# A five-stage transformer kernel: experts with four chunks in flight, and attention's constants and first loads made in earlier stages

## The reference, cut to what matters

```python
mod = (silu(L0_c) @ L0_wmod)            # six rows of 256 per sequence: shift, scale, gate, twice
x = x + ga * attention(layernorm(x) * (1 + ca) + sa)   # 16 heads of 16, ALiBi bias, causal
x = x + gb * fp4_swiglu(layernorm(x) * (1 + cb) + sb)
mod = (silu(L1_c) @ L1_wmod)
x = x + ga * state_space(layernorm(x) * (1 + ca) + sa)
h = layernorm(x) * (1 + cb) + sb
# experts: six of rank 16, the two with the largest softmax weight are used
base_out, shared_out = h @ base_W.T + base_b, (h @ shared_A.T) @ shared_B.T
gate = softmax(h @ router_W.T + router_b)            # [.., 6]
sparse_w = top2(gate) / (sum(top2(gate)) + 1e-6)
routed = sum_e sparse_w[e] * (h @ routed_A[e].T) @ routed_B[e].T
x = x + gb * (base_out + shared_out + routed)
```

## Time and profile before

| what | value |
|---|---|
| median of three runs | 4541.62 us (4540.84 to 4541.89) |
| the profiled execution | 4536.81 us, its span 4535.0 us |
| setup | 0 to 37.6 us |
| projection | 37.6 to 249.1 us |
| attention | 249.1 to 1416.9 us |
| experts | 4219.6 to 4535.0 us |
| TensorE busy over the span | 78% |
| VectorE busy | 79% |
| GpSimd busy | 53% |
| ScalarE busy | 50% |

### The profile page before, as it was taken

How to read it: one execution, slowest core, us unless ns; L and a number is a source line. 1 busy time by engine, 2 the same in 40 slices (tenths; PEclk the granted TensorE clock), 3 DMA queues, 4 the chain that set the end, 5 groups by cost and what they waited for, 6 DMA issues and landing times. The chain is left out here.

```text
span 4535.0 us, 73462 instructions
## 1 busy us (share of the span) xinstructions
PE 3538.0 (78%) x23500; PEld 1707.1 (38%) x23500; DVE 3567.3 (79%) x5194; ACT 2248.1 (50%) x3972; POOL 2406.5 (53%) x1812
## 2 busy tenths in 40 slices
PE   6949999999995899999567777777777777775566
PEld 3614444444442555555222222222222222221455
DVE  4767777777773899999289999989998999999344
ACT  3606666666664333333365665556565666564111
POOL 1120000000000788887278888888888888888121
PEclk8969999999997899999778888888887888885777
DMA  4864545545532111110112222222222122222111
GB/s 155 279 111 61 79 63 74 79 63 75 78 44 56 52 47 42 46 43 26 47 38 58 64 63 57 61 65 56 56 63 64 54 53 52 55 52 56 50 59 53
DMA packets 274028, 300.57 MB, mean 66 GB/s; under 512 B 34559, under 2 KB 204662, under 8 KB 273622
## 3 DMA queue, kind: packets, MB, share of 16 engines
q1 hardware_dynamic: 273630, 295.68, 29.7%
HBM read 210.22 MB, written 84.51 MB: 65 GB/s over the span
## 5 line engine op out<-in xcount | busy, mean ns | idle before, releaser
L1648 POOL TENSOR_TENSOR d_dBu<-d_dtu,d_Bn 128x1024 f32<-128x1024 f32 x512 | 1202.5, 2374 | 185.7 <-DVE d_h L1715 185.5
L749 DVE TENSOR_REDUCE b_Gc<-b_pS 128x1 f32<-128x512 f32 (+4 forms) x1248 | 748.8, 645 | 297.1 <-PE b_pS L630 189.2
L1496 ACT ACTIVATE d_dA<-d_dt,d_decay 128x512 f32<-128x512 f32 x1024 | 690.3, 687 | 448.7 <-DVE d_h L1715 431.9
L712 ACT ACTIVATE b_P<-b_pT 128x512 f32<-128x512 f32 (+1 forms) x1120 | 583.3, 575 | 397.5 <-PE b_pT L618 233.7
L1715 DVE TENSOR_TENSOR_SCAN d_h<-d_dA,d_dBu 128x512 f32<-128x512 f32 x512 | 586.2, 1204 | 96.9 <-ACT d_dA L1496 85.2
L1715 DVE TENSOR_TENSOR_SCAN d_h<-d_dA,d_last_h,d_dBu 128x512 f32<-128x512 f32 x512 | 616.5, 1264 | 54.7 <-ACT d_dA L1496 50.2
L584 POOL CAST b_gp<-b_gT 32x128 bf16<-32x128 f32 x32 | 9.0, 280 | 1032.3 <-ACT b_gT L696 1032.3
L628 PE MATMUL b_pS<-b_KS,b_QS 99*128 99x512 bf16 (+3 forms) x1536 | 473.4, 338 | 89.6 <-DMA b_V<-scratch_v 64.3
L616 PE MATMUL b_pT<-b_QS,b_KS 102*128 102x512 bf16 (+3 forms) x1536 | 470.7, 330 | 37.3 <-issue 20.9
L1722 DVE TENSOR_TENSOR d_h<-d_h,d_C 128x2048 f32<-128x2048 f32 x192 | 434.3, 2262 | 0.5 <-PE d_C L1379 0.5
L1451 PE MATMUL d_f<-d_xnT,w_inT 128*128 128x512 f32 x512 | 327.1, 773 | 128.0 <-DVE d_h1e L1782 59.8
(11 more groups left out here) (294 smaller groups left out, 6253.5 us busy)
## 6 DMA issues: line engine op xcount, KB each, us to landing
d_Bn<-scratch_bs SPq DMA_DIRECT2D x64, 1024.0 KB, 8.2
scratch_parts<-a_part SPq DMA_DIRECT2D x48, 512.0 KB, 4.0
b_QS<-scratch_parts SPq DMA_DIRECT2D x192, 128.0 KB, 7.0
b_KS<-scratch_parts SPq DMA_DIRECT2D x192, 128.0 KB, 7.3
scratch_v<-a_v SPq DMA_DIRECT2D x16, 1024.0 KB, 7.4
b_V<-scratch_v SPq DMA_DIRECT2D x32, 512.0 KB, 11.1
a_x<-in_L_attn_x_dram SPq DMA_DIRECT2D x16, 512.0 KB, 7.5
scratch_o<-b_O SPq DMA_DIRECT2D x16, 512.0 KB, 10.8
```

Of the source, the lines that this page charges most:

```text
L712: act.activation(t[:, heads[0]:heads[-1] + 1, c * CH:c * CH + w], pT[:, place % RING, 0:len(heads) * w].rearrange("p (h w) -> p h w", w=w) ...
L749: dve.tensor_reduce(Gc[:, m.k % 2, c, :].rearrange("p (h t) -> p h t", t=QT)[:, heads[0]:heads[-1] + 1, qt], pS[:, j % RING, 0:len(heads) ...
L1496: act.activation(dA[:, m % 2, :], dt[:, c.k % 2, m, :], ACT.Exp, scale=decay[:, m, n:n + 1]).then_inc(dA_d, 1)
L1648: pool.tensor_tensor(dBu[:, n % 2, 2 * j:2 * j + 2, :], dtu[:, c.k % 2, 2 * j:2 * j + 2, :], Bn[:, n // BG % 2, n % BG, :].unsqueeze(1).to ...
```

## The change

It has two parts, in stages that are far apart.

**Attention's constants and first loads.** `QS`, `KS`, `V` and `alp` are allocated ahead of `setup`. In `setup` SyncE loads the table between the loads of `c` and `wmod`, VectorE splits it, and ScalarE writes the ones (two copies of 6 partitions by 16384 elements). In `project_qkv`'s second step, behind the load of chunk 2, SyncE issues the 12 transfers from `alp` to `KS`. In its last step, ahead of the last chunk's stores, SyncE issues the 13 transfers of unit 0. `attend` starts with the load of unit 1.

```diff
--- setup
+            sp.dma_start(al[:, :], A["alibi"]).then_inc(al_in, 16)
+            act.wait_ge(one_set, 1)
+            for rows in (K["QS"], K["KS"]):
+                rows = rows[NROW:KROWS, :, :, :].rearrange("p g h t -> p (g h t)")
+                act.activation(rows, one[NROW:KROWS, :].to_broadcast(rows.shape), ACT.Copy).then_inc(ones, 1)
--- project_qkv, SyncE's step
                 if f is not None and (not isinstance(f.base, int) or f.base * U + f.k + 1 < total):
                     load(At(f.base, U, f.k + 1))
+                if f is not None and isinstance(f.base, int) and f.base == 0 and f.k == 1:
+                    for g_ in range(NG):
+                        for p in range(NPART):
+                            sp.dma_start(K["KS"][NROW + p:NROW + p + 1, g_, :, :], K["alp"][g_ * HG * QT:(g_ + 1) * HG * QT, p, :]).then_inc(S["alp_put"], 16)
+                if f is None and g is None:
+                    for sl in range(2):
+                        sp.wait_ge(stored[sl], 64)
+                    load_unit(sp, S, K, 0, 0)
--- attend
-            sp.wait_ge(ones, 2)
-            sp.wait_ge(al_step, 5)
-            for g in range(NG):
-                for p in range(NPART):
-                    sp.dma_start(KS[R0 + p:R0 + p + 1, g, :, :], alp[g * NQ:(g + 1) * NQ, p, :]).then_inc(alp_put, 16)
-                if u is None and m.k == 0:
-                    load(m)
-            pool.memset(QS[R0:KROWS, :, :, :].rearrange("p g h t -> p (g h t)"), 1.0).then_inc(ones, 1)
-            pool.memset(KS[R0:KROWS, :, :, :].rearrange("p g h t -> p (g h t)"), 1.0).then_inc(ones, 1)
```

```diff
+        LAG_G, LAG_D, LAG_C = 1, 2, 3
+        def chunks(step):
+            for s in range(total + LAG_C):
+                step(*(s - lag if 0 <= s - lag < total else None for lag in (0, LAG_G, LAG_D, LAG_C)))
--- TensorE: transposes of hw(c), transposes of xn(g), output products of c, hidden products of g
+                if c is not None:
+                    wait(pe, hw_d, 2 * c + 2)
+                    wait(pe, hwT_d, c)
...
+                    last.then_inc(hw_tr, 1)
+                if g_ is not None:
+                    wait(pe, xn_d, g_ + 1)
+                    wait(pe, hT_d, g_)
...
+                    last.then_inc(tr_d, 1)
+                if c is not None:
+                    wait(pe, hwT_d, c + 1)
+                    wait(pe, og_d, c)
...
+                    last.then_inc(o_mm, 1)
+                if g_ is not None:
+                    wait(pe, hT_d, g_ + 1)
+                    wait(pe, hw_d, 2 * g_ - 2)
...
+                    last.then_inc(a_mm, 1)
--- ScalarE: Exp of d, hwT of c, xn of f
+                if d is not None:
+                    wait(act, soft, NSOFT * (d + 1))
+                    act.activation(ex[:, d % 2, :, :], lg[:, :, :], ACT.Exp).then_inc(ex_d, 1)
+                if c is not None:
+                    wait(act, hw_tr, c + 1)
+                    wait(act, o_mm, c - 1)
+                    act.activation(hwT[:, c % 2, :], p_hw[0:NHW, :], ACT.Copy).then_inc(hwT_d, 1)
```

More of the change, by code:

```diff
@@ L1858, in _ @@
-            chunks(sp, step)
-            for i in range(4):
-                sp.wait_ge(stored[i], 16 * total // 4)
+                wait(sp, stored[n % XS], n // XS * 16)
+                sp.dma_start(x[:, n % XS, :, :], S["x3"][n * CH:(n + 1) * CH, :].rearrange("(t p) d -> p t d", p=P)).then_inc(x_in[n % XS], 16)
+                if n % 2 == 0:
+                    wait(sp, og_d, n - 2 * (GS - 1))
+                    sp.dma_start(gate[:, n // 2 % GS, :], S["mod"][n // 2:n // 2 + 1, 1, GB, :].to_broadcast([P, D])).then_inc(g_in[n // 2 % GS], 16)
@@ new lines, in step @@
+            def step(f, g_, d, c):
+                if f == 0:
+                    load(0)
+                    load(1)
+                if f is not None and f + 2 < total:
+                    load(f + 2)
+                if c is not None:
+                    wait(sp, out_d, c + 1)
+                    sp.dma_start(out[c * CH:(c + 1) * CH, :].rearrange("(t p) d -> p t d", p=P), x[:, c % XS, :, :]).then_inc(stored[c % XS], 16)
+            chunks(step)
+            for i in range(XS):
+                sp.wait_ge(stored[i], 16 * total // XS)
@@ L1862, in _, with step @@
         @block.tensor
         def _(pe):
-            def step(a, c):
-                if a is not None:
-                    wait(pe, xn_d, a.times(1, 1))
-                    wait(pe, hT_d, a.times(1, 0))
+            def step(f, g_, d, c):
+                if c is not None:
+                    wait(pe, hw_d, 2 * c + 2)
+                    wait(pe, hwT_d, c)
+                    for t in range(CT):
+                        last = pe.transpose(p_hw[0:NHW, t * P:(t + 1) * P], hw[:, c % 2, t, :], K["ident"][:, :])
+                    last.then_inc(hw_tr, 1)
+                if g_ is not None:
+                    wait(pe, xn_d, g_ + 1)
+                    wait(pe, hT_d, g_)
@@ L1912, in _, with step @@
-            chunks(act, step)
+            chunks(step)
         @block.gpsimd
         def _(pool):
-            pool.wait_ge(const, 9)
-            def step(a, c):
-                if a is not None:
-                    sl = a.k % 2
-                    wait(pool, stat, a.times(2, 2))
-                    wait(pool, xn_d, a.times(1, -1))
+            pool.wait_ge(const, 8)
+            def step(f, g_, d, c):
+                if f is not None:
+                    sl = f % 2
+                    wait(pool, stat, 2 * f + 2)
+                    wait(pool, xn_d, f - 1)
@@ L2010, in _ @@
-            chunks(dve, step)
+                if d is not None:
+                    wait(dve, ex_d, d + 1)
+                    picked(dve.tensor_reduce(sm[:, :], ex[:, d % 2, :, :], AX.X, ALU.add))
+                    pick_wait()
+                    picked(dve.reciprocal(sm[:, :], sm[:, :]))
+                    pick_wait()
+                    picked(dve.tensor_tensor(g[:, :, 0:NE], ex[:, d % 2, :, :], tiles(sm[:, :], NE), ALU.mult))
+                if g_ is not None:
+                    b = g_ // 2
+                    wait(dve, tr_d, g_ + 1)
+                    wait(dve, o_mm, g_ - HS_ + 1)
+                    dve.tensor_scalar(hT[:, g_ % HS_, 0, :], p_tr[:, 0, :], K["cb1"][:, 0, b:b + 1], K["sb1"][:, 0, b:b + 1], ALU.mult, ALU.add)
```

268 lines of the change are left out of this document (124 added, 144 removed).

## The result

The changed kernel takes 4375.98 us (median of 4 runs, 4365.23 to 4378.46), the kernel before 4541.23 (4 runs, 4534.00 to 4541.89). The ratio is 0.9635, with a 95% interval of 0.9616 to 0.9654: 165 us less, where 163 were predicted, and inside the range.

What follows compares the result with a forecast made beforehand. No engine bounds the two places: attention's start is a serial chain, an experts step a chain of dependencies. Experts -122.2, attention's start -41.4, setup +0.5 make -163.1 us; from 4541.6 that gives 4378.5, rounded to 4379, range 4359 to 4413.

Steps and rivals of the forecast that it cites:

- the six links: Experts: loop from og through GpSimd's addition, held subtraction, Exp, hwT and output products to next og, 10.18 us a step.
- The sixth: Experts, link from Exp to hwT: Exp 0.22 us and 0.04 to the hwT behind it, 0.26.
- the fill: Experts' start before the steady steps: first lg at 4237.54, second at 4245.8, then 14 full steps.
- the first full step: Experts: no addition to wait for but low clock, estimated 11.4 us (2.6 + 7.27 + 1.5).
- The subtraction is held: Experts: GpSimd's addition holds VectorE's subtraction to its end, 1.53 us long; without the hold 9.6 a step.
- the swing: Rival, experts: TensorE's clock swings between levels; 4417 us at clock 0.73, 4481 at the lower level throughout; chance 0.14.
- TensorE idle for over 2.5 us a step: Experts: a sign that would prove the forecast wrong; the predicted break was 1.6 us in 10.2.
- The constants' part: Attention's start: fills, table, casts and constants' transfers leave the time before the first matmul; with unit 0's loads 41.4 gained.
- The serial queue: Projection's end: unit 0's 15.9 us of loads fill 2.7 idle, push last stores 13.2; boundary 249.1 to 262.3.
- the stores are issued at most 1.3 us late: Projection's end: SyncE's 13 issues of unit 0 take 8.2 us, delaying the issue of the stores at most 1.3.
- Unit 1's load: Attention: issued at 262.3, lands near 280, covered by unit 0's maxima; without cover at most 17 us waiting.
- the constants' twelve puts: Projection's second step: twelve transfers, 7.59 us of SyncE's time, taken to cost 0; if wholly exposed, 7.6 once.

Runs made afterwards that it cites:

- the kernel without it (8.36): Changed kernel with the router's maximum and its subtraction left out, Exp taking the bare logits: 4347.28 us, ratio 0.9572.
- the one that takes it off the loop (8.66): Changed kernel with ScalarE's copy hwT of chunk c ahead of Exp of chunk d: 4351.86 us, ratio 0.9590.
- the two kernels made with 3.48 and 5.43: Changed kernel with hwT also waiting for the next chunk's rs (3.48): 4427.56 us; with hwT last in ScalarE's step, behind xn (5.43): 4461.94 us.

## Why the prediction was right

**Experts, -126.2 for -122.2.** Five of the six links stand within 0.02 us of what was taken from the earlier trace rows. The sixth was mis-sized: `Exp` to `hwT` is 0.13, not 0.26, for in the trace `hwT` starts 0.13 us behind `Exp`, ahead of its end. So the step is 10.05 and not 10.18, 1.7 us over 13 steps. The rest lies in the fill, where the first full step took 9.7 and not the estimated 11.4. That estimate has a slip in it: 1.97 us for 8 transposes make 3.0 and not 2.6 for 12; at full clock the 12 take 1.5. The subtraction is held and ends with GpSimd's addition, as said; it lasts 0.94 us and not 1.53 as it starts later in it. That this link decides is shown twice, by the kernel without it (8.36) and by the one that takes it off the loop (8.66). The Trainium skill, GPSIMD Engine Reference, section 1 (Specifications), names instructions of two SBUF inputs as those that contend with GpSimd. The changed trace agrees: `lg`, with one of its inputs in PSUM, lasts 0.17 us while the addition runs, and the subtraction, with both in SBUF, 0.93. That the addition is what holds it is read from the ends: started 0.26, 0.85 or 1.45 us behind the addition (2.13, 1.53 and 0.93 us long), the subtraction ends 0.03 to 0.04 us behind it, and it takes 0.16 where no addition runs. No run took the addition away.

**The clock, 0.92 over the stage.** It was expected over 0.9. The prediction gave the swing 0.14 on the strength of the earlier trace rows and named TensorE idle for over 2.5 us a step as what would prove it wrong. The changed kernel has 1.51, and the two kernels made with 3.48 and 5.43 show what would then have come.

**Attention's start, -43.3 for -41.4.** The constants' part went as read. The serial queue was a fair model: the boundary came at 260.2, not at 262.3. Unit 0 was through at 252.3 (its last transfer, issued at 240.36, lands 11.9 us later), 14.3 us behind the store ahead of it (229.86 + 8.1 = 238.0), where the prediction took 15.9 from the rate of 132 GB/s. The spread loads fit the model too, which fills idle time of the engines. Two things are missing in it. SyncE's own time is one: 13 issues behind the last stores cost 4.8 us, nearly all of it issuing. And "the stores are issued at most 1.3 us late" fell short: the parts' are 2.4 us late and take SyncE 9.12 us. I read that as the queue being full, which no run isolated. It didn't matter, since the engines had no room either. Unit 1's load hindered nothing that can be told: it lands at 277.9 in the changed kernel, while unit 0's maxima keep VectorE without a break from 261.71 to 283.0. Attention, from its first matmul to the next stage, is 1111.5 to 1117.4 us long in the profiles of kernels with the change's attention, 1113.2 and 1118.0 in those without.

**Setup and the constants' twelve puts.** Setup is 37.4 to 39.0 us, on the mean of the twelve kernels with the new one 38.0, against 37.6 and 38.0 in the two with the old: +0.2 for the +0.5 predicted, both less than the 1.6 by which equal setups differ. The fills are 13.84 us each, the slope from the earlier trace rows to 0.1, and the puts cost nothing: with them, and with the loads spread, projection is as long as before.

**What stays open.** Why state space differs by 20 us between executions of unchanged code. Its spread, not the change, decides the last 10 us of any total here. Open is also why three stores took SyncE 9.12 us to issue.

## What to carry to other kernels

When a pipeline is deepened, follow the loop that remains from a result to the same result one step on. Look on every in-order engine for an operation of the loop that stands behind one of another chunk: swapping two instructions on ScalarE was worth 21 us here, where removing the slow operation itself, and the maximum before it, was worth 24. A transfer that is moved ahead of a stage boundary is hidden only where the DMA engines have room; spread it over the stretch before. In front of the last stores it delays their landing, and behind them the engine that issues it comes late to the boundary. Removing a break of TensorE pays twice once the break is short enough to keep the clock: 18.4 us a step fell to 10.05 and the same 832 matmuls took 50 us less, while a break of 3.5 us lost the clock again in every step.

## What the runs showed of the hardware

Twelve transfers of 16 partitions keep the DMA engines full (share 1.07 from 237 to 241 us) at 128 GB/s, where the stores left alone ran at 361 with a share of 0.98: a full DMA share says nothing of the rate. With the 13 loads in the queue ahead of them, three stores took SyncE 9.12 us to issue in place of 2.03. A break of 1.5 us in each 10 us leaves TensorE's granted clock at 1.00, one of 3.48 us in 13.7 brings it down for 3.3 us of every step, one of 5.43 in 17.1 for 6.8. And the hold that VectorE suffers beside GpSimd's addition lasts to the end of that addition: a subtraction of 24 elements a row takes 0.16 us alone and 0.93, 1.53 or 2.13 us by when it starts.
